# A graph network layer in two parts: the first tiles of seven node groups are summed in the first part, one a step

## The reference

```
h     = relu(layernorm(x))
msg   = relu(relu([h[src], h[dst], edge_attr] @ Wm1 + bm1) @ Wm2 + bm2)     one row for each edge
agg   = segment_sum(msg, dst, 50000)
u     = relu([h, agg] @ Wu1 + bu1)
out   = x + h + u @ Wu2 + bu2
```

## Time and profile before

| | |
|---|---|
| runs | 800.0 us median (798.3 to 801.7) |
| the profiled execution | 800.28 us, of which the span is 798.4 us |
| part 1, up to the last eviction | about 531 us |
| part 2 | about 267 us |
| busy over the span | PE 87%, DVE 85%, ACT 79%, POOL 71% |
| DMA moved | 184.56 MB, 231 GB/s over the span |
| granted TensorE clock | 0.998 of full speed |

### The profile page before, as it was taken

The page is one execution under the profiler, slowest core; times in us unless marked ns, Lnnn a source line. Parts: engine busy times, 40 slices in busy tenths (PEclk is TensorE's granted clock), DMA queues, the critical chain, the costliest instruction groups (busy, mean ns, idle before and its releaser), DMA issues.

```text
span 798.4 us, 18682 instructions
## 1 busy us (share of the span) xinstructions
PE 694.5 (87%) x3154; PEld 414.7 (52%) x3155; DVE 676.5 (85%) x2269; ACT 630.5 (79%) x1434; POOL 563.7 (71%) x784
## 2 busy tenths in 40 slices
PE   0398999999988888888888888889999999999997
PEld 0244444444444444434444444445778778776765
DVE  2798888988888888888888888769999998998886
ACT  0588888888888888888888888756788888888886
POOL 7777777777777777777777777639777656655542
PEclk9999999999999999999999999999999999999999
DMA  5466666666666666666666665450579999999998
GB/s 153 119 212 217 215 217 220 228 223 216 217 217 208 199 205 213 213 209 201 199 203 210 213 217 184 149 211 14 172 228 271 335 339 330 368 346 348 360 355 292
DMA packets 99727, 184.56 MB, mean 231 GB/s; under 512 B 15101, under 2 KB 16512, under 8 KB 99700
## 3 DMA queue, kind: packets, MB, share of 16 engines
q1 hardware_dynamic: 46628, 81.69, 30.5%
q10 hardware_dynamic: 40528, 76.89, 26.9%
q0 software_dynamic: 12544, 25.72, 12.0%
HBM read 107.25 MB, written 76.98 MB: 231 GB/s over the span
## 4 chain that ended last, share of the span: by engine, by line
DMA 38%; PE 20%; issue 19%; DVE 7%; POOL 6%; ACT 4%; DVEq 2%; ACTq 2%; SPq 1%; POOLq 1%
DMA xg<-x_in,ends_all 36%; PE bank L871 7%; PE bank L905 5%; POOL xg L318 5%; PE bank L872 5%; DVE hot L769 2%; ACT zn L506 1%; DVE xg L446 1%; DVE hu_i L792 1%; DVE xh_o L803 1%; ACT high L823 1%; ACT dist L832 1%; POOL low L739 1%; DVEq L171 1%; DMA hu_i<-hu_scratch 1%
## 5 line engine op out<-in xcount | busy, mean ns | idle before, releaser
L318 POOL DMA_INDIRECT xg<-x_in,ends_all x392 | 392.9, 1002 | 119.9 <-DMA xg<-x_in,ends_all 104.5
L739 POOL TENSOR_TENSOR low<-msgs,high 128x128 fp32r<-128x128 f32 x303 | 153.0, 520 | 88.1 <-ACT high L823 84.2
L506 ACT ACTIVATE zn<-xn,shift,rstd 128x128 f32<-128x128 f32 x392 | 160.5, 483 | 2.0 <-DVE shift L423 1.8
L871 PE MATMUL bank<-hot,low 128*128 128x512 f32 x303 | 136.1, 449 | 10.3 <-DVE hot L769 3.9
L769 DVE TENSOR_SCALAR hot<-node,dst_f,minus_base 128x512 fp32r<-128x512 f32 x229 | 131.3, 619 | 15.6 <-PE bank L872 11.7
L381 DVE BATCH_NORM_STATS2 bn<-xg 128x6 f32<-128x128 f32 x392 | 80.5, 278 | 51.8 <-DMA xg<-x_in,ends_all 51.8
L872 PE MATMUL bank<-hot,high 128*128 128x512 f32 x303 | 119.6, 395 | 0.0
L609 PE MATMUL bank<-ident,xg 128*128 128x128 f32 x392 | 64.5, 288 | 54.8 <-DVE xg L446 54.8
L625 PE MATMUL bank<-ht,w_uh 128*128 128x512 f32 x196 | 106.1, 623 | 2.9 <-ACT ht L525 1.9
L446 DVE TENSOR_SCALAR xg<-xg,rstd,shift 128x128 f32<-128x128 f32 x392 | 107.3, 357 | 0.1
L905 PEld LDWEIGHTS bank<-w_out,u_t 128*128 128x128 f32 x784 | 99.1, 191 | 15.4 <-issue 7.1
(11 more groups left out here) (72 smaller groups left out, 1001.8 us busy)
## 6 DMA issues: line engine op xcount, KB each, us to landing
hu_i<-hu_scratch SPq DMA_DIRECT2D x98, 256.0 KB, 4.4
xh_i<-xh_scratch SPq DMA_DIRECT2D x98, 256.0 KB, 4.4
out<-xh_o SPq DMA_DIRECT2D x97, 256.0 KB, 4.4
hu_scratch<-ht ACTq DMA_DIRECT2D x48, 512.0 KB
xh_scratch<-xh_o ACTq DMA_DIRECT2D x48, 512.0 KB
xn<-x_in ACTq DMA_DIRECT2D x44, 512.0 KB, 3.7
xg<-x_in,ends_all POOLq DMA_INDIRECT x392, 2.8
edge<-edge_t_in ACTq DMA_DIRECT2D x45, 64.0 KB
```

Of the source, the lines that this page charges most:

```text
L318: pool.indirect_dma_start(xg[:, slot, t, :], None, x, bass.IndirectOffsetOnAxis(ap=ends_all[:, s, t:t + 1], axis=0), engine_sem=s_made).th ...
L506: ins = act.activation(zn[:, slot % 2, t - 8, :], xn[:, slot, t - 8, :], ACT.Relu, bias=shift[:, slot % 2, t:t + 1], scale=rstd[:, slot % ...
L739: return pool.tensor_tensor(low[:, at, :], msgs[:, k, :], high[:, at, :].bitcast(F32), ALU.subtract)
L871: pe.matmul(to, low[:, at, :], hot[:, at, :], start=start, stop=False, skip_group_check=True)
```

## The change

While part 1 runs, a tile's sum over its group can already be made, as soon as its messages are there. EARLY = (16, 8, 4, 4, 4, 4, 4) is the most tiles that groups 0 to 6 may give; together 44, which is one tile for each of the steps 4 to 47. Four tiles of one group are a unit; there are 11.

- **The table** works out how many of these each group really gives (all but two at most, and only if they lie early enough in the order), moves the start of the group's range in part 2 by that number, and writes the list of early tiles; an entry that isn't used points at a tile of zeros. TABLE goes from 18 to 43. SP moves the list through DRAM as well, with one store and three loads (s_early).
- **In each step 4 to 47**: ACT copies the tile to high_e (`early_high`), DVE makes hot_e (128x512) and low_e (128x128) (`early_parts`, between its normalising and the statistics of the fetched rows), and PE adds both products into a bank p_early (`early_sum`, between L648 and the transposes of the nodes).
- **After each fourth**: DVE adds the bank to hu_e, which SP has loaded from the scratch of that group, and SP stores it back (`add_early`). In part 2 this hu is loaded as before.
- **Banks**: p_m1 and p_m2 become one bank p_m, so that p_early has one; in the last two steps the second layer uses p_early.
- **SBUF**: the integer tables of the setup now lie in hu_i, and hu_e lies in slot 0 of xh_i. So SP's first loads of part 2 wait for the last unit's store as well.

```diff
+EARLY = (16, 8, 4, 4, 4, 4, 4)
+GROUP_OF = [g for g, n in enumerate(EARLY) for _ in range(n // 4)]
...
+            def early_tile(self, slot, use):
+                if slot == 0:
+                    self.eng.load(self.early, early[0:1, bass.ds(4 * use - 4, 4)])
+                return self.eng.snap(self.early[slot], min_val=0, max_val=ET)
...
SyncE
+                for unit, g in enumerate(GROUP_OF):
+                    if unit:
+                        sp.wait_ge(s_est, 16 * unit)
+                    sp.dma_start(hu_e, hu_d[g]).then_inc(s_eld, 16)
+                    sp.wait_ge(s_eadd, unit + 2)
+                    sp.dma_start(hu_d[g], hu_e).then_inc(s_est, 16)
...
+                sp.wait_ge(s_esum, 1 + 4 * UNITS)
+                sp.wait_ge(s_est, 16 * UNITS)
                 for g in range(4):
                     load_hu(sp, g, g)
...
VectorE, part 1
+                def early_parts(s, slot, use):
+                    dve.wait_ge(s_esum, s - 3)
+                    k = tiles.early_tile(slot, use)
+                    dve.tensor_scalar(hot_e[:], node[:], dst_f[:, bass.ds(k, 1)],
+                                      minus_early[:, bass.ds(use - 1, 1)], ALU.subtract, ALU.is_equal).then_inc(s_ehot, 1)
+                    dve.wait_ge(s_ehi, s - 3)
+                    dve.tensor_tensor(low_e[:], msgs[:, k, :], high_e[:].bitcast(F32), ALU.subtract).then_inc(s_elo, 1)
+                def add_early(use):
+                    dve.wait_ge(s_esum, 1 + 4 * use)
+                    dve.wait_ge(s_eld, 16 * use)
+                    dve.tensor_tensor(hu_e, p_early[:], hu_e, ALU.add).then_inc(s_eadd, 1)
...
+                    if at_least(s, 4) and below(s, STEPS - 1):
+                        early_parts(s, slot, use)
                     if below(s, STEPS):
                         stat_of_ends(s, slot, use)
+                    if at_least(s, 4) and below(s, STEPS - 1) and slot == 3:
+                        add_early(use)
...
ScalarE, part 1, after w_h(s - 1, prev, 0)
+                def early_high(s, slot, use):
+                    act.wait_ge(s_esum, s - 3)
+                    act.wait_ge(s_msgs, s - 3)
+                    k = tiles.early_tile(slot, use)
+                    act.activation(high_e[:], msgs[:, k, :], ACT.Copy).then_inc(s_ehi, 1)
...
TensorE, part 1, after msg_of(s - 2)
+                def early_sum(s, slot, use):
+                    pe.wait_ge(s_ehot, s - 3)
+                    pe.wait_ge(s_elo, s - 3)
+                    if slot == 0:
+                        pe.wait_ge(s_eadd, use)
+                    pe.matmul(p_early[:], low_e[:], hot_e[:], start=slot == 0, stop=False, ...)
+                    pe.matmul(p_early[:], high_e[:], hot_e[:], start=False, stop=slot == 3, ...).then_inc(s_esum, 1)
...
-            p_tr, (p_m1, p_m2, p_msg, p_hu) = banks[0:4], banks[4:8]
+            p_tr, p_m, p_early, p_msg, p_hu = banks[0:4], banks[4], banks[5], banks[6], banks[7]
```

More of the change, by code:

```diff
@@ L1 @@
+import itertools
 from contextlib import ExitStack
@@ L81, in build @@
         ranges = sb("ranges", [1, GROUPS * 2], I32)
+        early = sb("early", [1, 4 * UNITS], I32)
+        minus_early = sb("minus_early", [P, UNITS])
         msgs = sb("msgs", [P, ET + SPARE, D])
@@ L144, in __init__ @@
                 self.in_pair = [eng.alloc_register(f"{name}_in_pair{i}") for i in range(2)]
+                self.early = [eng.alloc_register(f"{name}_early{i}") for i in range(4)]
+            def early_tile(self, slot, use):
+                if slot == 0:
+                    self.eng.load(self.early, early[0:1, bass.ds(4 * use - 4, 4)])
+                return self.eng.snap(self.early[slot], min_val=0, max_val=ET)
             def begin(self):
@@ L194, in build @@
             ident = sb("ident", [P, P], on=one)
[L195 to L199, removed]
+            ends_all = hu_i[:, 0, 0:8 * STEPS].bitcast(I32).rearrange("p (s t) -> p s t", t=8)
+            rows_i = hu_i[0:ET // 2, 1, 0:2 * P].bitcast(I32).rearrange("q (k e) -> q k e", k=2)
+            dst_i = hu_i[:, 2, 0:ET + SPARE].bitcast(I32)
+            minus_i = hu_i[:, 3, 0:GROUPS].bitcast(I32)
             ext = sb("ext", [ET // 2, 2, 2], on=one)
@@ L204, in build @@
             rng_i = sb("rng_i", [GROUPS, 2], I32, on=one)
+            early_i = sb("early_i", [GROUPS, EARLY[0]], I32, on=one)
+            most, from_lo, taken = (sb(n, [GROUPS, 1], on=one) for n in ("most", "from_lo", "taken"))
             bn = sb("bn", [P, 2, 16, 6], on=one)
@@ L212, in build @@
             m1t, m2t = sb("m1t", [P, W], on=one), sb("m2t", [P, W], on=one)
+            hot_e = sb("hot_e", [P, W], F32R, on=one)
+            high_e, low_e = sb("high_e", [P, D], F32R, on=one), sb("low_e", [P, D], F32R, on=one)
             spare = zn[:, 0, :, :].rearrange("p t d -> p (t d)")
@@ L284, in sync_1 @@
                 sp.dma_start(ranges[:], rng_d.rearrange("(o g) c -> o (g c)", o=1)).then_inc(s_rng, 16)
+                sp.dma_start(early_d, early_i[0:len(EARLY)]).then_inc(s_early, 16)
+                sp.wait_ge(s_early, 16)
+                at = 0
+                for n, rows in itertools.groupby(range(len(EARLY)), lambda g: EARLY[g]):
+                    rows = list(rows)
+                    sp.dma_start(early[0:1, at:at + n * len(rows)].rearrange("o (g c) -> o g c", c=n),
+                                 early_d[rows[0]:rows[-1] + 1, 0:n].rearrange("(o g) c -> o g c", o=1)
+                                 ).then_inc(s_early, 16)
+                    at += n * len(rows)
+                for half in range(2):
+                    sp.wait_ge(s_sto[half], 64)
+                for unit, g in enumerate(GROUP_OF):
[4 more added lines that the diff above has]
+                    sp.dma_start(hu_d[g], hu_e).then_inc(s_est, 16)
                 for half in range(2):
@@ L341, in start_table @@
                 did(dve.tensor_scalar(last[:], base_i[:], float(LAST), float(W - 1), ALU.min, ALU.add))
+                for unit, g in enumerate(GROUP_OF):
+                    did(dve.memset(minus_early[:, unit:unit + 1], -float(g * W)), False)
+                did(dve.memset(most[:], 0.0))
+                for n in sorted(set(EARLY)):
+                    did(dve.memset(most[0:sum(m >= n for m in EARLY)], float(n)))
+                did(dve.memset(from_lo[:], float(ET - 60)))
+                did(dve.memset(from_lo[0:1], float(ET - 3)))
             def finish_table(dve, did):
@@ L665, in body @@
                         msg_of(s - 2)
+                    if at_least(s, 4):
+                        early_sum(s, slot, use)
                     transposes_of_nodes(s, slot)
```

73 lines of the change are left out of this document (53 added, 20 removed).

## The result

The changed kernel takes 780.6 us (median of 4 runs, 779.9 to 781.5) against 800.85 (798.3 to 802.7): a ratio of 0.975, 95% interval 0.972 to 0.978. Forecast were 780. The profiled execution has a span of 778.2 us, 20.2 less than before.

What follows compares the result with a forecast made beforehand. Fetches were taken to bound part 1, DVE the first groups of part 2 and groups 7 to 13, DMA the later ones; 800.3 + 4 - 24 = 780.3, so 780 us, range 773 to 799.

Steps and rivals of the forecast that it cites:

- What bounds part 1: Part 1: it ends when POOL's stream of fetches ends; the loop has 0.7 us a step to spare.
- The stream, +3.5 us: Part 1's fetches: hot_e and low_e stretch them by 0.08 us a step, so step 48 starts at 511.8 for 508.29.
- The 0.09 us for each us of DVE: Part 1's fetches: each us of DVE's two-input or faster-copy work on SBUF stretches them by 0.09 us.
- rival B: Part 1: hot_e and low_e block the fetches for their whole time, +33 us, 809 us; chance 0.10.
- The loop, 10.3 us a step: Part 1: the loop grows from 9.74 to 10.3 us a step (10.1 to 10.8), step 48 starting at 511.5.
- The start, nothing: Setup: eight more small table instructions, 1.6 us, are covered by ACT's wait for the last weight; uncovered +1.6.
- Part 2, -24 us: Early groups of part 2: 44 fewer visits at 0.592 us of DVE, less some 2 us showing in group 0's chain.
- Rival C: Part 2, groups 7 to 13: loads meet a fuller DMA queue and 8 us return, 788 us; chance 0.09.
- A: Part 1: additions lie one behind the other and the loop becomes the bound, +23 us, 799; chance 0.08.
- D: Early tiles aren't taken because the condition fails: cost without gain, 804 us; chance 0.02.
- +4 in part 1: Part 1's whole cost: stream and loop end level, with 0.5 us added for their alternating.
- 511 to 514: Part 1: a sign that the forecast is right, the start of step 48 in us.

Runs made afterwards that it cites:

- cost_alone: Changed kernel with all its new work in part 1, but zero one-hots and part 2's ranges not shortened: 804.6 us, ratio 1.0056.
- gain_alone: Changed kernel without the new work per step in part 1; longer table, merged bank and shorter part 2 ranges stay: 777.4 us, ratio 0.972.
- hot_twice: Changed kernel with each step's one-hot made twice, the second into a buffer nobody reads: 791.8 us.
- sum_later: Changed kernel with PE's early sum behind the transposes of the nodes instead of before them: 772.1 us, ratio 0.965.
- xh_split: Changed kernel with each of DVE's two additions of x and h cut into two of 128x256: 800.4 us.
- before_xh_split: Kernel before the change, with only DVE's additions of x and h each cut in two: 808.3 us, ratio 1.014.
- add_in_wait: Changed kernel with PE's early sum behind the node transposes and DVE's addition to hu moved into the next step, before the reciprocal: 777.0 us.
- two_groups: Changed kernel in which only groups 0 and 1 give early tiles, the other units working on zeros: ratio 0.988 to the kernel before.

## Why the prediction was right
**What bounds part 1.** Right, and tighter than I had put it. From the start of fetch 384 to the first high part it is 27.1 us before, 27.3 after, and 26.8 to 27.5 in cost_alone, gain_alone, hot_twice, sum_later, xh_split, before_xh_split and add_in_wait, whose fetch 384 starts anywhere from 502.8 to 527.3. The end of part 1 is the stream of fetches and a constant, and the stream is 481.8 us and the fetches' losses.

**The stream, +3.5 us.** The sum was about right, its rule was not, and that the two met is luck. 19 fetches started within hot_e in the changed kernel and lost 3.5 us in all, 0.18 each; fetch 384 came 4.9 us later, the rest being mostly small losses beside the normalising (0.8 us) and the additions of b_out (0.3). The 0.09 us for each us of DVE is a mean over instructions that mostly miss and sometimes hold a fetch for nearly all that is left of them. I had also read a row wrongly: the fetch of 1.07 us, which I took for one beside other work, starts in the first addition of b_out, 0.25 us before its end. Doubling the one-hot showed the rule's failure: 0.5 us more of DVE a step cost 11 us and not 2 to 4. The Trainium skill's rule (SBUF — State Buffer, "Who interferes with whom"), "fully blocks", describes the single held fetch (1.36, 1.58 us), and the traces agree with it there. The 33 us that I drew from it for rival B were far off, since they took it that every new instruction meets a fetch for its whole length, and most don't. How far the meeting can shift with an edit is seen in the starts of fetch 384, 504.2 us before: 507.8 with none of the new work (gain_alone), 511.8 with nothing but x plus h cut (before_xh_split), and from the changed kernel's 509.1 to 502.8 by moving PE's sum and to 527.3 by cutting x plus h.

**The loop, 10.3 us a step.** Measured 10.14. PE's pair took 0.55 us (305.19 to 305.74 in the trace), DVE's pair 0.66, and DVE's wait for the root fell from 0.90 to 0.43 to 0.78, as the step had it. The two bounds were not quite level: from step 36 on DVE waited for rows in most steps, up to 1.9 us. That the loop grew by PE's sum in the chain is shown only in part: sum_later took the sum out of it, most steps got shorter, and the wait in the fourth gave it back.

**The start, nothing.** Nearly. Step 1 started 0.9 us later (29.39 for 28.51), and step 4 3.1 us later; 2.3 of these came in step 3 (12.15 us for 9.88), behind a first message layer whose six matmuls took 5.3 us instead of 3.1. It need not be the change's: step 3 of before_xh_split, without any of it, takes 13.45 us, and sum_later, with all of it, takes 9.86. Nothing was lost by it in the end, since the loop still caught up.

**Part 2, -24 us.** Right: 24.4 in the profiles, 24.0 between two timed kernels. The way to it, 44 x 0.592 less 2 us, is borne out by two_groups in its first factor: 25 visits gave 0.62 each, DVE's full price and a little more. But the 2 us are not lost where I had put them, in the chain of group 0: the last 19 visits, of groups 2 to 6, gave about 0.47 each. DVE is then no longer the full engine. I had worked out 20 us for it up to hu of group 6, from 22 one-hots and 12 additions; the stretch did take 20.5, but with 15 one-hots and 11 additions, 14.4 us of work, and 7.0 us of waiting for PE's first bank. PE was busy 18.7 us. So this length is right and its bound is not, and no run shows what would shorten it. Rival C, DMA, took nothing: from hu of group 6 on the time is 0.9 us less, not more. Rivals A, B and D did not come.

**+5.1 and not +4 in part 1.** Step 48 started at 514.4 us, just outside my 511 to 514, and DVE's waits for rows, 1.0 us on the mean of steps 42 to 48, didn't fall to 0.5. All of the 5.1 but 0.2 us is longer fetches. How much of that is the new work and how much a shifted meeting with the old additions, the runs leave open: gain_alone had fetch 384 3.6 us late with none of the new work, sum_later had it 1.4 us early with all of it. What edit moves the meeting which way I can't foretell; neither of my guesses on it (xh_split, add_in_wait) came true.

The version with the sum behind the transposes, 772.1 us, beats both kernels and is the one to keep. That it does so by when its fetches happen to start, and not by its loop (10.12 us for 10.14), should be kept in mind when anything ahead of it is edited.

## What to carry to other kernels
Work moved out of a full stretch is worth the full engine's time for each piece only until the next limit shows; count it there, and look in the other stretch for the engine that sets its end, not for the one that gets busier. Where the end is set by a stream that meets another engine's instructions, a mean rate of interference is no price: it is the start times that decide, so a small edit can be worth more by its shift than by its work, and a result of 1% needs a look at how many of the stream's pieces were held.

## What the runs showed of the hardware
A fetch by POOL of 128 rows takes 0.94 us. One that starts while DVE runs an addition with two SBUF inputs goes on when that addition ends and takes what was left of it, less 0.12 us, on top (722 of 777 fetches, to 0.03 us). If a second addition stands back to back with the first, 174 of 221 fetches still went on at the first's end and 47 only at the second's (2.07 us). A fetch that starts within 0.02 us of the addition's start lost nothing, and the addition of 128x512 then took 0.72 to 0.74 us for 0.69. A fetch that starts 0.10 us before the end of a one-hot (128x512, one SBUF input) with low_e behind it lost 0.18 us, and 0.64 with a second one-hot between them, but 0.04 where it started 0.08 us before the one-hot. A row of eight 128x128 instructions of one input, 2.2 us in all, costs a fetch that starts in it 0.03 to 0.05 us on the mean. With all additions cut to 32 columns the mean fetch was 948 ns.
